# A four-layer graph network on one core: the second and last layer's pass with the back stages two to three batches later

## What is computed

```
# second layer
pre    = h[src] @ W_q + h[dst] @ W_k + edge_attr @ W_e + biases
score  = leaky_relu(pre) @ a_w + a_b
alpha  = softmax of score over the edges of one dst
out    = segment_sum(alpha * (h[dst] @ W_v), dst)
# fourth layer (4 active rules)
score[e, r] = ((q[dst] . key_base[src, type]) + q[dst] . key_rule[r]) / 8
attn   = softmax over the edges of one dst, mean over r
out    = segment_sum(attn * (h[src] @ W_r[type]), dst), layernorm, relu
```

## Time and profile before

| what | value |
|---|---|
| median of 3 runs | 8520.82 us (8500.45 to 8528.5) |
| the profiled execution's own time | 8492.32 us |
| its span, first to last instruction | 8490.5 us |
| DVE busy over the span | 4832.2 us, 57% |
| POOL busy over the span | 4967.0 us, 59% |
| PE busy over the span | 5200.4 us, 61% |
| ACT busy over the span | 4211.9 us, 50% |
| granted TensorE clock, mean | 0.736 |

### The profile page before, as it was taken

One profiled execution on the slowest core, in us unless ns is written; L12 is line 12 of the kernel. 1 busy time (PEld: TensorE's weight loads), 2 busy tenths in 40 slices (PEclk: granted clock), 3 DMA queues, 4 the chain that ended last, 5 costly groups with the idle time before them and its releaser, 6 DMA issues. The chain is left out here.

```text
span 8490.5 us, 161453 instructions
## 1 busy us (share of the span) xinstructions
PE 5200.4 (61%) x38193; PEld 3779.8 (45%) x38194; DVE 4832.2 (57%) x21267; ACT 4211.9 (50%) x11643; POOL 4967.0 (59%) x5713
## 2 busy tenths in 40 slices
PE   4666666666664444444444448997666666666664
PEld 3555555555552222222222226885444444444443
DVE  5555555554545555555555568996555555555556
ACT  3445555554523434343433348994554555555554
POOL 5555555555535555555555547994555666565663
PEclk8888888887876666666666668998676666676666
DMA  4233333333334444444444446885222222222221
GB/s 116 83 87 87 87 87 87 88 86 86 87 90 128 128 129 128 126 129 129 128 128 126 128 120 218 267 268 205 59 62 60 63 63 63 61 63 62 63 63 42
DMA packets 672779, 908.53 MB, mean 107 GB/s; under 512 B 141174, under 2 KB 429928, under 8 KB 672441
## 3 DMA queue, kind: packets, MB, share of 16 engines
q1 hardware_dynamic: 502366, 605.50, 23.0%
q0 software_dynamic: 168944, 301.30, 14.6%
q10 hardware_dynamic: 1357, 0.47, 0.0%
HBM read 696.57 MB, written 210.28 MB: 107 GB/s over the span
## 5 line engine op out<-in xcount | busy, mean ns | idle before, releaser
L785 POOL DMA_INDIRECT rows<-src_rows,idx_slots x1563 | 1499.0, 959 | 1172.3 <-DVE pre L1504 600.5
L785 POOL DMA_INDIRECT rows<-rel_rows,idx_slots x1563 | 1499.3, 959 | 1022.5 <-issue 409.8
L785 POOL DMA_INDIRECT rows<-node_rows,idx_slots x1371 | 1310.2, 956 | 999.4 <-issue 366.7
L1391 ACT ACTIVATE onehot<-ident,fresh_slots 128x128 f32<-128x128 f32 x3136 | 992.9, 387 | 899.2 <-remote 643.4
L1382 PE MATMUL bank<-onehot,ones 128*128 128x512 f32 x1568 | 1304.1, 928 | 4.3 <-ACT onehot L1391 4.3
L1480 PE MATMUL bank<-w_e,edge_in 128*128 128x256 f32 x784 | 427.3, 645 | 1402.7 <-DVE onehots L867 945.4
L1089 ACT ACTIVATE dst_pairs<-pre,minus_node 128x512 bf16<-128x512 int16 x816 | 577.6, 719 | 1145.7 <-remote 757.9
L1480 PEld LDWEIGHTS bank<-w_e,edge_in 128*128 128x128 f32 x784 | 189.6, 293 | 1855.0 <-issue 938.0
L1119 PE MATMUL bank<-by_chunk,dst_pairs 128*128 128x192 bf16 x6144 | 791.3, 275 | 260.8 <-issue 145.4
L1119 PE MATMUL bank<-wide_room,dst_pairs 128*128 128x192 bf16 x3264 | 488.8, 283 | 548.7 <-ACT dst_pairs L1093 472.4
L1191 DVE TENSOR_SCALAR dst_pairs<-pre,node_at 128x512 bf16<-128x512 int16 x1536 | 545.9, 355 | 467.2 <-remote 309.2
(11 more groups left out here) (307 smaller groups left out, 12151.2 us busy)
## 6 DMA issues: line engine op xcount, KB each, us to landing
edge_in<-dst_line SPq DMA_DIRECT2D x392, 256.0 KB
spill<-rows SPq DMA_DIRECT2D x392, 256.0 KB
rows<-spill SPq DMA_DIRECT2D x392, 256.0 KB, 3.2
hot_rows<-rows SPq DMA_DIRECT2D x98, 712.0 KB
onehots<-hot_rows SPq DMA_DIRECT2D x196, 356.0 KB, 3.5
onehots<-src_low SPq DMA_DIRECT2D x98, 512.0 KB
edge_in<-in_ea_l SPq DMA_DIRECT2D x98, 256.0 KB
edge_in<-in_eaT_l SPq DMA_DIRECT2D x392, 64.0 KB
```

The source lines that it names most:

```text
L785: pool.indirect_dma_start(out=to[:, b.slot(ROW_RING), g, :], out_offset=None, in_=table, in_offset=bass.IndirectOffsetOnAxis(ap=idx_slots[ ...
L1391: last = act.activation(diag[:, b.slot(2), g, :], ident[:, :], ACT.Copy, scale=fresh_slots[:, b.slot(2 * RING), g:g + 1])
```

## The change

Only the lags and one order are changed, in the two sweeps. Second layer: on every engine each stage but `hot` (0) and `look` (1) comes two steps later. Last layer: the lags of `scores`, the diagonal, the mask, `spread`, the maximum and its parts, `find`, `shrinks` and `build` grow by two; those of `take`, `differ`, `clamp`, `exps`, `weigh`, `sum_up` and `add` grow by three; and DVE's list is put in another order, in which `take`, `differ`, `clamp` and `add`, which stood behind `low`, stand between `maxima` and `low`. POOL's and SP's lists are not touched.

```
 # score_sweep
-pipeline(act, [(3, spread_stage(...)), (3, far_stage(...)), (5, exps)])
+pipeline(act, [(5, spread_stage(...)), (5, far_stage(...)), (7, exps)])
-pipeline(pe, [(1, look), (4, spread)])
+pipeline(pe, [(1, look), (6, spread)])
-pipeline(dve, [(5, maxima), (7, sums), (5, largest), (2, join), (5, running),
-               (2, leak), (5, tops), (0, hot), (5, biases), (2, scores)])
+pipeline(dve, [(7, maxima), (9, sums), (7, largest), (4, join), (7, running),
+               (4, leak), (7, tops), (0, hot), (7, biases), (4, scores)])
 # attention_sweep
-pipeline(act, [(2, far_stage(...)), (3, shrinks), (2, spread_stage(...)), (4, exps), (4, weigh)])
+pipeline(act, [(4, far_stage(...)), (5, shrinks), (4, spread_stage(...)), (7, exps), (7, weigh)])
-pipeline(pe, [(1, look), (5, sum_up), (3, find), (2, spread)])
+pipeline(pe, [(1, look), (8, sum_up), (5, find), (4, spread)])
-pipeline(dve, [(3, maxima), (3, running), (3, high), (3, left), (0, hot), (3, middle), (3, low),
-               (1, scores), (3, take), (3, differ), (5, add), (0, build), (3, clamp)])
+pipeline(dve, [(5, maxima), (6, take), (5, running), (6, differ), (5, high), (6, clamp),
+               (5, left), (0, hot), (5, middle), (8, add), (5, low), (3, scores), (2, build)])
```

More of the change, by code:

```diff
@@ L1467, in exps @@
                                .then_inc(s_exp, 1)
-                        pipeline(act, [(3, spread_stage(act, s_score, s_diag, s_spread)),
-                                       (3, far_stage(act, far1, RING, s_hot, s_far, s_masked)),
-                                       (5, exps)])
+                        pipeline(act, [(5, spread_stage(act, s_score, s_diag, s_spread)),
+                                       (5, far_stage(act, far1, RING, s_hot, s_far, s_masked)),
+                                       (7, exps)])
                     @block.tensor
@@ L1648, in weigh @@
                             last.then_inc(s_weighted, 1)
[L1649 to L1652, removed]
+                        pipeline(act, [(4, far_stage(act, far3, 2, s_hot, s_far, s_spread)),
+                                       (5, shrinks),
+                                       (4, spread_stage(act, s_score, s_diag, s_spread)),
+                                       (7, exps), (7, weigh)])
                     @block.tensor
@@ L1792, in _ @@
                         split_table(dve, Chain(dve, s_chain), D + N_ACTIVE, N_ACTIVE, s_table, s_took)
[L1793 to L1796, removed]
+                        pipeline(dve, [(5, maxima), (6, take), (5, running), (6, differ), (5, high),
+                                       (6, clamp), (5, left), (0, hot), (5, middle), (8, add),
+                                       (5, low), (3, scores), (2, build)])
                         dve.wait_ge(s_added, N_BATCHES)
```

## The result

| | median of the runs, us | ratio, 95% interval |
|---|---|---|
| before | 8524.66 (8500.45 to 8534.72, 4 runs) | |
| after | 8573.39 (8565.44 to 8583.67, 4 runs) | 1.0066 [1.0047, 1.0084] |

The change made the kernel 0.66% slower; the forecast was 1.1% faster. The profiled span is 8563.7 us, the granted clock 0.720 in the mean instead of 0.736.

A forecast was written before the change was run, and what follows sets the result against it. No single engine bounds the sweeps; order and waits do, with POOL's gathers as a 1954 us floor. Terms 5 + 47 + 29 - 180 + 5 = -94 us took 8520.8 to 8427, forecast as 8425 us (-1.1%), range 8100 to 8650.

The forecast's parts named there:

- Its rings of buffers: Last layer's sweep: row slots still suffice, `add` waits for `sum_up` at no extra cost; the longer sweep end costs 5 us.
- the ring: Last layer's sweep: low, find, spread, maxima and back to low, 4.04 us at 2.4 GHz, about 5.1 us at 1.2 GHz.
- the 0.12: Last layer's sweep: both rings get 0.12 us longer a step from the operations moved between `maxima` and `low`.
- 0.4 us of air: Last layer's sweep: slack in the ring through `find`, expected to absorb 0.4 of about 0.5 us added.
- The pauses, -180 us: Last layer's sweep: waits ahead of `scores` and `take` go, saving 180 us, ends 0 and 501 us.
- nothing moves: Rival: gathers and pauses set the sweeps' pace, so DVE's gains return as longer waits; about 8520 us, chance 0.17.
- The rings, +47 and +29 us: Last layer's sweep: operations moved into the rings cost +47 us, the late window load moving with `add` +29 us.
- the bubble end: Last layer's sweep: low end of the rings' cost, the moved operations all falling into bubbles, 0 us.
- The end from the Trainium skill: Last layer's sweep: high end of the rings' cost, interleaving fills nothing and full durations are paid, +149 us.
- The window load: Last layer's sweep: the late load moves with `add` into the ring, 49 times 0.6 us, +29 us, ends 0 and +65.
- The second layer, +5 us: Second layer's sweep: a uniform shift keeps all distances but look to join; +5 us, ends -8 and +13.
- Longer rings: Rival: the four moved instructions cost full durations in every step, pauses only move; about 8700 us, chance 0.25.

The follow-up runs named there:

- e4: The kernel before, all its lags kept, with only `add` put ahead of `low` in DVE's list of the last sweep: 8585.15 us, ratio 1.009.
- e1: The changed kernel with `add` moved behind `low` and `scores` in DVE's list of the last sweep, lag kept: 8514.05 us, ratio 1.000.
- e5: The kernel before, its last sweep gathering only two of each batch's four tiles: 7882.47 us, ratio 0.9133.
- e7: The changed kernel with `add` behind `low`, its last sweep gathering only two of each batch's four tiles: 7873.22 us, ratio 0.9135.
- e9: The kernel before, its last sweep gathering three of each batch's four tiles, on another chip: 6549.82 us, ratio 0.9745.
- e13: The changed kernel with `add` moved behind `low`, run again on another chip, which had the pauses: 8523.23 us, ratio 1.0006.
- second run: The kernel before with only the second layer's lags changed, run again in a later set: 8521.16 us, ratio 1.0006.
- e15: The changed kernel with all its gathers, on a chip that turned out to have no pauses: 6734.07 us, ratio 1.0021.
- e6: The changed kernel, its last sweep gathering only two of each batch's four tiles: 7942.0 us, ratio 0.9212.
- e3: The kernel before with only the last layer's lags and order changed: 8585.9 us, ratio 1.008.

## Why the prediction was wrong

**The step that failed first** is the sentence on `add` under "Its rings of buffers": "In the ring sum_up ends about where `add` starts; I put nothing on it beyond the 0.12." I had named the wait and what is queued behind it, and priced it at nothing from one step with PE at 2.4 GHz. `maxima` and PE's look start together. Behind look and `sum_up` at 1.2 GHz `add` starts 3.63 us after `maxima` (7006.35 to 7009.98 above), where DVE had reached it after 2.02 (it waited 1.61). The price is 1.8 us of a step that had 0.4 us of air; e4 alone makes 1.009, e1 without it 1.000. The traces of e5 to e7 split the 1.8 us. At the higher clock, from which I had read the step, it is 0.15 us, so the 0.12 was right there; 0.6 us more comes with the lower clock; 1.0 us is the late increment of `sum_up`. Rows 5 had shown such lateness, and I had counted it as pauses only, not as a wait that a moved `add` would put into every step. In the mean step it comes to 0.16 us (63 us a sweep), because pauses shrink for it; on the order's own pace, without pauses, the changed order costs 36 to 70 us. The lower mean clock of the sweep (0.62, 0.63 in e4) goes with this chain and not with the lags (0.70 in e1); how much of the 0.66% comes from that drop alone the runs don't separate.

**The pauses, -180 us, came to nothing.** The signs were all forecast and came (idle ahead of L1705 and L1764 gone, L1714 up), but the inference from them was wrong. I had charged each pause with DVE's work behind it, as if the pause ended at a fixed time. e1 has that distance, and 494 us of waits there turned into 501 us elsewhere. My rival "nothing moves" had the mechanism right: what a shorter order wins comes back as a wait while POOL issues gathers back to back. e5 shows that the pauses of its sweep need the full number of gathers; whether it is their issue on POOL or their DMA traffic, halving both does not tell. e9 shows that they need the chip, or its surroundings, as well: the same untouched second layer's sweep took 1953 us there and 2583 elsewhere.

**The rings, +47 and +29 us**, were too high. `maxima` to L1734 is 1.14 us after and was 1.15, with `take` and `differ` between; the bubble end, 0, was right. The end from the Trainium skill ("VectorE: DVE Perf Modes", "The DRAIN you can't avoid"), by which such interleaving fills nothing, did not come. I had used its rule that the next operation waits for the empty pipe, and left out the sentence behind it, "A next op that is not held starts earlier"; in the timeline after, L1723 and L1770 start 0.08 us apart and last 0.16 and 0.15 us, so the trace agrees with that sentence. The window load can't be told from zero: e1 holds it, and all its terms together came to 0.0% (e13 +0.06%).

**The second layer, +5 us with ends at -8 and +13**: 1.0022 and 1.0006, that is +19 us (9 to 28) and +5 us (-8 to +18); `join` waited 1.4 us instead of 8, and that gained nothing measurable. The +5 is right as far as the second run can tell; the first lies at or above the upper end.

**Mistaken in size besides**: `maxima` to `low` 3.83 instead of 2.4 to 2.6; the wait ahead of L1714 591 us instead of some 450; POOL's waits on L1689 and "remote" 685 us, where 500 was forecast. I had listed "`add` waiting for L1689" as what would show the forecast wrong, and its row shows 299 us under that name and 310 as "remote".

"Longer rings", the rival that ended slower, had the right sign with the wrong cause: `take`, `differ` and `clamp` cost nothing (2.04 us from `maxima` to `low` in e1), `add` by itself at most the 0.15 us above; the wait inside it cost everything.

## What to carry to other kernels

An instruction moved ahead of the head of a ring brings its wait along: price it as the time at which the producer's increment arrives, at the lower clock, minus the time at which the engine gets there, and not by its duration. Where the traces show late increments, take the arrival from steps of that kind and not from modelled ends: here 3.6 us instead of 2.6. Long waits with no releaser near them are not won by distance between the stages; take away half of what runs during them (here the gathers) to see the order's own pace before reordering. Before tuning against such pauses, run the kernel before on more than one chip.

## What the runs showed of the hardware

- The same kernel took 8513 to 8633 us on two chips (8513 and 8633 in two sets on the same one) and 6722 to 6726 us on two others. Nearly all of the difference is in the sweeps that gather: for the changed kernel 1178 of 1830 us in the two that the change touches (2569 to 1957 and 2519 to 1953 us), most of the rest in the first layer's. In the second layer's, idle ahead of L1529 was 910 us and is 10 us in e15, with POOL's gather 0.95 to 0.96 us long in both. Whether it is the chip or what else ran beside it, the runs don't say.
- In e15, on a chip without pauses, POOL issues gathers 1.25 us apart for a whole sweep (1953 us) and no long wait there is put down to "remote"; so back-to-back gathers alone don't make the pauses, though in e5 to e7, on a chip with pauses, halving them removed the pauses of that sweep.
- On the chips with pauses the semaphore of `sum_up` moves late in nearly every step of the full sweep: 1.42 us (median) behind PE's modelled end in the changed kernel, against 0.01 us in e6 (the chip of e3 and e4, half the gathers) and in e15 (all gathers, another chip). The lower clock is not the cause: at a granted clock of 0.5 `add` starts 0.2 us behind the modelled end in e6 and e15 and 1.2 us behind it in the changed kernel. What delays it the runs don't show.
